# Leaf mask and first bias of a hard-routed feed-forward: out of the matmul, into an SBUF ring added by DVE

## The reference, cut to what matters

```python
def _fff(x, node_w, node_b, w1, b1, w2, b2):      # once each for q, k, v
    ...                                           # 4 levels of a tree: leaf = 0..15 per token
    sel = jax.nn.one_hot(leaf, N_LEAVES)
    hidden_all = jax.nn.relu(jnp.einsum('nd,ldh->lnh', xf, w1) + b1[:, None, :])
    hidden = hidden_all * sel.T[:, :, None]       # 16 leaves x 64 = 1024 hidden rows, 15 of 16 masked
    return jnp.einsum('lnh,lho->no', hidden, w2) + sel @ b2

attn = softmax(q @ k.T / sqrt(128)); ffn = attn @ v
x = x + 0.5 * ffn(layernorm(x))                   # "ffn"
x = x + mha(layernorm(x))                         # "mha", 16 heads, rope, alibi, causal
x = x + 0.5 * ffn(layernorm(x))                   # "ffn" again
x = x + 0.5 * moe(layernorm(x))                   # "moe", 8 experts, top 2
x = x + mamba(layernorm(x))                       # "mamba"
x = x + 0.5 * moe(layernorm(x))                   # "moe" again
```

## Time and profile before

| | |
|---|---|
| median of 3 runs | 1534.77 us (1529.73 to 1534.88) |
| the profiled execution | 1534.62 us |
| its span, first to last instruction | 1532.8 us |
| mean granted TensorE clock over the span | 0.919 |
| PE, DVE, ACT, POOL busy | 82%, 66%, 39%, 16% of the span |

### The profile page before, as it was taken

How to read it: one execution, slowest core, us unless ns; L and a number is a source line. 1 busy time by engine, 2 the same in 40 slices (tenths; PEclk the granted TensorE clock), 3 DMA queues, 4 the chain that set the end, 5 groups by cost and what they waited for, 6 DMA issues and landing times.

```text
span 1532.8 us, 16423 instructions
## 1 busy us (share of the span) xinstructions
PE 1253.6 (82%) x5768; PEld 755.4 (49%) x5768; DVE 1012.4 (66%) x1988; ACT 594.4 (39%) x991; POOL 239.2 (16%) x200
## 2 busy tenths in 40 slices
PE   5996858899899565769999967689989966657798
PEld 3674433577665122336667633336766632312465
DVE  6666646455575996977754664645556859879764
ACT  4542424343323555422234415253442253455222
POOL 3001000000010361531000010000001005526110
PEclk9998989999999697879999979799999987969799
DMA  5213040000000000000000120300000000000000
GB/s 198 56 41 76 4 97 3 1 0 1 1 1 0 1 0 0 0 0 1 8 21 1 42 57 23 77 3 1 1 1 1 1 0 0 0 0 1 0 7 7
DMA packets 22578, 28.16 MB, mean 18 GB/s; under 512 B 3072, under 2 KB 18720, under 8 KB 22304
## 3 DMA queue, kind: packets, MB, share of 16 engines
q1 hardware_dynamic: 22496, 27.11, 6.6%
HBM read 19.57 MB, written 8.06 MB: 18 GB/s over the span
## 4 chain that ended last, share of the span: by engine, by line
PE 61%; DVE 21%; issue 8%; ACT 5%; DMA 3%; SPq 1%; POOL 1%; DVEq 0%; ACTq 0%; POOLq 0%
PE bank L1266 11%; PE bank L1268 11%; PE bank L1267 11%; PE bank L1436 8%; DVE n_h L1234 5%; DVE a_mx L1172 3%; PE bank L1345 3%; DVE bank L1226 3%; PE bank L1275 3%; PE bank L1493 2%; PE bank L1533 2%; PE bank L1401 2%; DMA a_k<-stack_dram 2%; PE bank L1474 2%; PE bank L1427 1%
## 5 line engine op out<-in xcount | busy, mean ns | idle before, releaser
L1031 DVE SCALAR_TENSOR_TENSOR f_hl<-bank,f_hh 128x512 fp32r<-128x512 f32 x192 | 131.8, 689 | 128.1 <-ACT f_hh L718 127.4
L718 ACT ACTIVATE f_hh<-bank 128x512 fp32r<-128x512 f32 x192 | 114.7, 597 | 199.3 <-PE bank L1345 198.8
L652 POOL TENSOR_TENSOR n_hc<-n_h,n_cs 128x512 f32<-128x512 f32 x128 | 160.8, 1272 | 141.2 <-DVE n_h L1234 87.0
L777 ACT ACTIVATE m_sl<-bank 128x512 f32<-128x512 f32 x144 | 85.8, 597 | 234.2 <-PE bank L1268 233.7
L1266 PE MATMUL bank<-xT_h,mw_h 128*128 128x512 f32 x288 | 161.3, 560 | 5.5 <-DVEq L450 4.3
L1583 PE MATMUL bank<-n_hc,ident 128*128 128x512 f32 x256 | 151.8, 715 | 11.0 <-POOL n_hc L652 10.2
L1234 DVE TENSOR_TENSOR_SCAN n_h<-n_da,bank 128x512 f32<-128x512 f32 x128 | 149.0, 1200 | 3.9 <-POOL n_hc L652 3.9
L1096 DVE TENSOR_TENSOR m_t<-m_sl,bank 128x512 f32<-128x512 f32 x128 | 87.9, 687 | 94.7 <-PE bank L1268 80.5
L597 POOL TENSOR_TENSOR small<-small,half 128x4 f32<-128x4 f32 x24 | 24.3, 1012 | 803.4 <-DVE small L934 803.0
L1436 PE MATMUL bank<-m_h,mw 128*128 128x512 f32 x288 | 145.4, 593 | 0.0
L854 ACT ACTIVATE n_da<-n_dt,amat 128x512 f32<-128x512 f32 x128 | 91.7, 721 | 132.3 <-DVE n_h L1234 125.3
(11 more groups left out here) (237 smaller groups left out, 2440.7 us busy)
## 6 DMA issues: line engine op xcount, KB each, us to landing
a_q<-stack_dram SPq DMA_DIRECT2D x8, 512.0 KB, 7.0
a_k<-stack_dram SPq DMA_DIRECT2D x16, 256.0 KB, 7.9
stage_fw<-in_fw_dram SPq DMA_DIRECT2D x6, 512.0 KB, 7.5
stack_dram<-R SPq DMA_DIRECT2D x16, 192.0 KB, 2.8
w_stage<-in_mw_dram SPq DMA_DIRECT2D x9, 256.0 KB, 2.7
stack_dram<-R SPq DMA_DIRECT2D x16, 128.0 KB, 2.6
mw<-in_mw_dram SPq DMA_DIRECT2D x1, 1152.0 KB, 8.2
X<-in_x_dram SPq DMA_DIRECT2D x4, 256.0 KB, 7.4
```

What stands on the lines that cost most here:

```text
L652: n_hcs.by(nc.gpsimd.tensor_tensor(n_hc[:, m, :], n_h[:, m, :], n_cs[:, n // 2 % 2, :], ALU.mult))
L718: f_hi.by(act.activation(f_h[0][:, i % 4, :], bank[:, i % 3, :], ACT.Relu))
L1031: f_lo.by(V.scalar_tensor_tensor(f_h[1][:, i % 4, :], bank[:, i % 3, :], 0.0, f_h[0][:, i % 4, :].bitcast(F32), ALU.max, ALU.subtract))
```

## The change

The bf16 matmul of `b1w` and `R` goes. In its place the mask is made a real number in `R` (the compare now also multiplies by -2^100), its 16 rows are written to `mask_dram`, and from there read back so that each leaf's row is spread over that leaf's 64 partitions: a ring `f_mask` of 4 steps in SBUF, loaded two steps at a time by two DMAs. Step i becomes: DVE writes `f_z` = bank + b1 (a column) + mask (L1071); ACT makes `f_h[0]` = Relu(f_z) and then Relu of f_z in place; POOL makes `f_h[1]` = f_z - f_h[0] (L652). The bank is now freed by DVE's add; `f_z` is a ring of 3, so DVE waits for POOL's step i - 3. The second product trails by 4 steps instead of 2. Each p = 1 ffn unit ahead of mha loads `rope` before its masks. POOL's "guess" for the next unit moves behind its low part of step 1 (p = 0) or 8 (p = 1).

```diff
-FFN_LAG = 7
+FFN_LAG, FFN_TRAIL = 7, 4
+MASK_RING, Z_RING = 4, 3
@@ SP
+            def masks(k, p, j):
+
+                at = 2 * j
+                if at >= MASK_RING:
+                    sp.wait_ge(f_zs.sem, f_zs.at(k, at - MASK_RING + 1))
+                elif k >= 1:
+                    sp.wait_ge(f_zs.sem, f_zs.at(k - 1, STEPS + at - MASK_RING + 1))
+                t, m = divmod(at, M1)
+                ring = at % MASK_RING
+                for half in range(2):
+                    sp.dma_start(f_mask[64 * half:64 * half + 64, ring:ring + 2, :],
+                                 mask_dram[p, t, 2 * m + half:2 * m + half + 3:2].unsqueeze(0).to_broadcast([64, 2, T])) \
+                        .then_inc(f_mld[ring // 2].sem, 16)
+                f_mld[ring // 2].made += 1
...
+                if kind == "ffn":
+                    if to_heads:
+                        a_rld.by(sp.dma_start(rope[:], A["rope"]))
+                    for t in range(TREES):
+                        sp.wait_ge(t_sel.sem, t_sel.at(k, t))
+                        f_mwr[t].by(sp.dma_start(mask_dram[p, t], R[0:LEAVES, p, t, :]))
+                    for j in range(STEPS // 2):
+                        sp.wait_ge(f_mwr[2 * j // M1].sem, f_mwr[2 * j // M1].at(k, 0))
+                        masks(k, p, j)
...
@@ POOL
                 if kind == "ffn":
-                    prologue(u + 1, "guess")
+                    for i in range(STEPS):
+
+                        pool.wait_ge(f_rl.sem, f_rl.at(k, i))
+                        f_lo.by(nc.gpsimd.tensor_tensor(f_h[1][:, i % 4, :], f_z[:, i % Z_RING, :],
+                                                        f_h[0][:, i % 4, :].bitcast(F32), ALU.subtract))
+                        if i == FFN_LAG * p + 1:
+                            prologue(u + 1, "guess")
@@ ACT
-                        act.wait_ge(f_s1.sem, f_s1.at(k, i))
+                        act.wait_ge(f_zs.sem, f_zs.at(k, i))
                         if i >= 4 or p == 1:
                             act.wait_ge(f_s2.sem, f_s2.at(k, i - 4))
-                        f_hi.by(act.activation(f_h[0][:, i % 4, :], bank[:, i % 3, :], ACT.Relu))
+                        f_hi.by(act.activation(f_h[0][:, i % 4, :], f_z[:, i % Z_RING, :], ACT.Relu))
+                        f_rl.by(act.activation(f_z[:, i % Z_RING, :], f_z[:, i % Z_RING, :], ACT.Relu))
@@ DVE
-                    dve.wait_ge(f_hi.sem, f_hi.at(k, i))
-                    f_lo.by(V.scalar_tensor_tensor(f_h[1][:, i % 4, :], bank[:, i % 3, :], 0.0,
-                                                   f_h[0][:, i % 4, :].bitcast(F32), ALU.max, ALU.subtract))
+                    dve.wait_ge(f_s1.sem, f_s1.at(k, i))
+                    dve.wait_ge(f_mld[i // 2 % 2].sem, f_mld[i // 2 % 2].at(k, i // MASK_RING))
...
+                    if i >= Z_RING or p == 1:
+
+                        dve.wait_ge(f_lo.sem, f_lo.at(k, i - Z_RING))
+                    f_zs.by(V.scalar_tensor_tensor(f_z[:, i % Z_RING, :], bank[:, i % 3, :], b1[:, i:i + 1],
+                                                   f_mask[:, i % MASK_RING, :], ALU.add, ALU.add))
@@ PE
-                for i in range(STEPS + 2):
+                for i in range(STEPS + FFN_TRAIL):
...
-                            pe.wait_ge(f_lo.sem, f_lo.at(k, i - 3))
+                            pe.wait_ge(f_zs.sem, f_zs.at(k, i - 3))
...
-                        product(b, [fw1[c][:, t, m * P:(m + 1) * P] for c in range(2)], x, stop=False)
-                        f_s1.by(mm(b, b1w[:, t, m * P:(m + 1) * P], R[:, p, t, :], start=False, stop=True))
-                    if i >= 2:
-                        i2 = i - 2
+                        f_s1.by(product(b, [fw1[c][:, t, m * P:(m + 1) * P] for c in range(2)], x))
+                    if i >= FFN_TRAIL:
+                        i2 = i - FFN_TRAIL
```

More of the change, by code:

```diff
@@ L173, in program @@
         col = sb("col", [P, 20])
-        leaf_thr, node_b, norm_w = (col[:, i:i + 1] for i in range(3))
+        leaf_thr, node_b, norm_w, leaf_scale = (col[:, i:i + 1] for i in range(4))
         conv_w = col[:, 5:13].rearrange("p (m c) -> p m c", m=NHALF)
@@ L339, in program @@
         e_row = sig("e_row", "moe", 1)
+        f_mwr = [sig(f"f_mwr_{t}", "ffn", 1, 16) for t in range(TREES)]
+        f_mld = [sig(f"f_mld_{n}", "ffn", STEPS // MASK_RING, 16 * 2) for n in range(MASK_RING // 2)]
         f_s1 = sig("f_s1", "ffn", STEPS)
+        f_zs = sig("f_zs", "ffn", STEPS)
+        f_rl = sig("f_rl", "ffn", STEPS)
         f_hi = sig("f_hi", "ffn", STEPS)
@@ L354, in program @@
         f_pv = sig("f_pv", "ffn", NT)
+        f_wtd = sig("f_wtd", "ffn", 1)
         r_hi = sig("r_hi", "once", 1)
@@ L494, in _ @@
             load(stage_b[:], A["bias"], bias_in)
-            load(block_of[:], A["block_of"], bias_in)
+            load(b1[:], A["b1"], bias_in)
             tree_weights(0, 1)
@@ L511, in _, with split_load @@
                     load(stack_dram[side, odd, MAX_ROW:], A[name][:, odd], rows_in)
-            for n, what in enumerate(SPLITS):
+            def split_load(n):
                 if n >= 2:
                     sp.wait_ge(w_lo.sem, w_lo.at(0, n - 2))
+                what = SPLITS[n]
                 src = A[what] if isinstance(what, str) else A["mw"][:, what * MW1:(what + 1) * MW1]
                 w_in[n % 2].by(sp.dma_start(split_src(n), src))
+            def masks(k, p, j):
[11 more added lines that the diff above has]
+                f_mld[ring // 2].made += 1
             for u, (kind, p) in enumerate(UNITS):
                 k = kth[u]
+                to_heads = kind == "ffn" and u + 1 < NU and UNITS[u + 1][0] == "mha"
+                if kind == "ffn":
[7 more added lines that the diff above has]
+                        masks(k, p, j)
+                        if k == 0 and j == 4:
+                            for n in range(2):
+                                split_load(n)
+                        if k == 0 and j >= 6:
+                            split_load(j - 4)
+                        if k == 1 and j in (1, 2, 6):
+                            split_load((1, 2, 6).index(j) + 8)
                 if kind == "mha":
@@ L611, in _ @@
             prologue(0, "guess")
-            pool.wait_ge(bias_in, 32)
-            pool.wait_ge(b_hi.sem, b_hi.at(0, 2))
-            for t in range(TREES):
-                expand(t)
             pool.wait_ge(early_in, 16 * NEARLY)
@@ L660, in bias_part @@
             def bias_part(first, src):
-                b_hi.by(act.activation(parts_b[first:P], src[first:P], ACT.Copy))
+                b_hi.by(act.activation(b2w[first:P], src[first:P], ACT.Copy))
             def tree_split(t, which):
@@ L878, in bias_rest @@
                 dve.wait_ge(b_hi.sem, b_hi.at(0, n))
[L879 removed]
+                b_lo.by(V.tensor_tensor(rest_b[first:P], src[first:P], b2w[first:P], ALU.subtract))
             def tree_split(t, which):
```

58 lines of the change are left out of this document (28 added, 30 removed).

## The result

The changed kernel takes 1636.26 us (median of 4 runs, 1632.48 to 1639.02) beside 1534.83 of the kernel before on the same chip: 1.067 times as long, 95% interval 1.063 to 1.070. The direction was forecast; of the 101 us the forecast had 52. The profiled execution spans 1636.0 us.

What follows compares the result with a forecast made beforehand. PE's own work was taken to bound the ffn units. The terms -44.7 + 39 + 17.6 + 26 - 2.6 + 5 + 6 + 6 gave +52, so 1587 us; range 1530 to 1618.

Steps and rivals of the forecast that it cites:

- Removed matmuls: One of seven matmuls gone in each of 192 ffn steps, 0.233 us each: -44.7 us if PE stays the bound.
- "Turn": PE waits 5.0 us for DVE's xn at "turn" in each of eight ffn units, less 0.15 each before: +39 us.
- The other waits: Further waits: +17.6 us in p = 0 units, +26 in p = 1; -2.6 for half-clock starts of k = 2 and 6.
- +6 for splits and residuals: DVE's weight splits in k = 0 and 1 and residuals ahead of mha, contending with POOL: 0 to 1.1 us each, +6.
- the walk: Both kinds of ffn unit followed with forecast durations, engines in program order; as it stands 1570 to 1605 us, chance 0.55.
- Clock: Half clock behind the eight 5 us turn waits: 0 to 2 us per wait, taken as 0.75 x 8 = +6.
- Start-up: In k = 0 the mask rows go to DRAM behind the start-up loads: +5 us, between 2 and 8.
- Masks in steady state: Mask loads of two steps, wanted 3.5 us after issue and taking 3.2, cost nothing.
- one of the forecast's signs of being wrong: DVE adds whose idle time ends with the mask's DMA, which would mean late masks.
- only turn waits: Rival, chance 0.17: turn waits 3.7 us in eight units, 5 at the start, everything else hidden; 1525 us.
- the waits merge: Rival, chance 0.14: lateness at "first" and slot 0's attention is caught up by PE's backlog, clock stays up; 1556 to 1565 us.
- Masks late: Rival, chance 0.12: broadcast mask loads land in 4.5 us or more, steps slow down, +15 to +35; 1602 to 1622 us.

Runs made afterwards that it cites:

- the experiment: The kernel before with its 192 mask matmuls left out and nothing put in their place: 1502.99 us, ratio 0.978.
- its experiment: The changed kernel with ACT's copies for the next unit's stack ahead of their step's Relus in k = 1 and 5: 1619.35 us.
- the filled turn: The changed kernel with 14 more matmuls ahead of PE's wait at turn in all eight ffn units: 1645.62 us.
- the run with one input: The changed kernel with PE reading the high part twice and POOL's unread instruction having one input (f_z times 1.0) instead of two: 1611.37 us.

## Why the prediction was right in direction and half in size

- **Removed matmuls, -44.7.** Nearly right as PE's own work (39.5 in the stretches, which held 42.9 of it). As time it was over-sized: the experiment gives 33. In the eight stretches PE's work falls by 38, idle time grows by 4 and half clock takes 6, most of it at the ends of k = 3 and 7. The condition "if PE stays the bound" was weakest there; the window of k = 3 above has PE at 42.17 of 47.90 us, and k = 5 in the earlier trace rows at 59.39 of 64: the idle 5 us were the sign.
- **"Turn", +39.** Measured 33.6 us of waits, by the chain foretold: guess behind the second or ninth low part, Newton's first multiply at 1.15. The price was right as idle time and wrong as a separate cost: moving it away gave 1 to 7 us. That DVE, ACT and POOL are themselves late by the same chain is my reading of it; the runs show only that the wait comes back elsewhere.
- **The other waits, +17.6, +26, -2.6, and +6 for splits and residuals.** With turn they make 86 us of idle time; 87.1 was measured. That is luck: the residuals ahead of mha were costed as contention alone, 0 to 1.1 each; the chain of 3.76 us a step, 17 us by its experiment, was not in the walk. Against that, turn was 5 less and other waits shorter, and a PE at half clock fills time in which it would have been idle.
- **Clock, +6: the step that failed.** "PE is then partly held by the adds anyway: 0 to 2 us per wait, I take 0.75 x 8". The 117 us of half clock in the stretches cost PE 48.8 us of work, 43 more than the term, and 43 is most of the 51 us between the forecast and the 103 of the profiled executions; 4.3 is the start of k = 4 and 5 the matmuls. It was counted for the eight turn waits alone, but the clock falls after other waits as well, down to 2.1 us long, and stays down for 3.4 to 13.7 us. Part of it is covered by waits, as the filled turn shows, and part is time of its own, 5.5 us at two places; how the rest divides no run here tells. The table above shows the same two parts in what the experiments took away.
- **Start-up, +5**: right, +4.3: the first add starts at 28.18 where the sum had 28.6. Without the masks' way it starts at 20.34, 7.8 us earlier, since the rest of the start got 3.6 us shorter. **The start of k = 4**, for which the sum had nothing: +4.3. SP's queue was not walked at that unit, and the store of X stands ahead of the masks there.
- **Masks in steady state, 0**: right as time; no stretch moved by more than 2.5 us without them. The margin was thinner than forecast: with the 2.9 us to landing in place of 2.6 the load takes 3.5 us, just the 3.5 it has, and nine adds did wait for it. That was one of the forecast's signs of being wrong; it showed and cost nothing that can be measured.
- **The Trainium skill's rule** on shared interfaces (GPSIMD Engine Reference, Key points), that POOL and a VectorE instruction with two SBUF inputs contend: the trace agrees at "turn", Newton's first multiply taking 1.15 us for 0.16 in all eight units, 1 us a wait as the rows had it. It matters more in the residuals, which have two SBUF inputs as the rule wants, and where I gave it 6 us with the splits; the run with one input says 17, what the clock does there included.
- Of the rivals, "only turn waits" and "the waits merge" failed by the clock and the chain ahead of mha. "Masks late", at 1602 to 1622, came nearest to the result for a reason that doesn't hold.

## What to carry to other kernels

When an element-wise step is taken from a bank that several engines read side by side and made a chain (add, clip, clip, subtract on three engines), look first at every place where one of these engines already waits in order for another: there each new link is paid in full, step after step, and engines at 40% busy are on the path. Then count all waits of PE of 2 us and more that the change makes, not only the longest, and price the clock behind each by what follows it: nothing if PE waits again soon, half the low stretch if it doesn't (a reading of three places here, not a rule that was tested). And before a matmul is removed, run the kernel without it: here that bound was 33 us of 44.7, in the stretches where PE was busy 88% it was 0.2, since the clock fell behind a wait there, and one run tells.

## What the runs showed of the hardware

- A DVE instruction with two SBUF inputs, started while a POOL instruction with two was at work, ended only after POOL's: the residuals 0.55 us after it (936.49 for 1.37 us above, POOL's ending at 937.31; eight of eight in k = 1 and 5), Newton's small first multiply 0.02 us after it. Beside a POOL instruction with one input of 1.49 us the same residual took 0.69 us, and the multiply 0.50 where it takes 0.16 alone. The add, with a bank, a column and one SBUF tensor, took 0.73 to 0.75 always. The Trainium skill, SBUF — State Buffer, "SBUF: two separate sides", has the first holder block the other for its whole instruction whenever POOL's reads SBUF; that agrees with the two-input case and not with the residuals beside one input.
- The clock fell to one half in or after PE waits of 2.1 to 4.7 us (2.1 us from 880.9, half from 883.5; 4.4 from 915.5, half from 917.7) for 3.4, 6.8, 10.2 or 13.7 us, but not after all of them (2.5 us from 379.9, no fall); the same wait of 3.7 us ahead of the expert weights was followed by 13.7 us in k = 3 and 3.4 in k = 7, and the stretches, with equal idle time (13.4 and 13.4 us), were 60.9 and 57.5 us long. The Trainium skill, TensorE: Matmul & The Clock Gate, "HAM oscillation", tells of a kernel whose bursts each start slow after a wait; the trace agrees, with waits shorter than those I had counted.
- A broadcast of one DRAM row of 1 KB to 64 partitions, two rows to a transfer of 128 KB, landed in 2.8 to 4.2 us, median 2.9, 192 times: no slower than a plain transfer of that size (2.6) to speak of.
